# The start of a fused Macaron block re-ordered around its ternary weights, and its last store cut in two

## The reference

```python
x = x + 0.5 * ffn(layernorm(x), W_up, W_gate, W_down)
x = x + mamba(layernorm(x), ...)        # 1024 channels, 16 states, a scan over the tokens
x = x + 0.5 * ffn(layernorm(x), W_up, W_gate, W_down)

def ternary_quant(w):                   # once for each of the three matrices
    scale = mean(|w|) + 1e-8
    return clip(round(w / scale), -1, 1) * scale
def ffn(x, W_up, W_gate, W_down):       # 512 -> 2048 -> 512
    return (silu(x @ wu.T) * (x @ wg.T)) @ wd.T
```

## Time and profile before

| | us |
|---|---|
| median of three runs | 2939.0 (2936.71 to 2941.12) |
| the profiled execution | 2940.29 |
| its span, first to last instruction | 2938.7 |
| granted TensorE clock, mean | 0.970 |
| busy: PE / PEld / DVE / ACT / POOL | 2657.0 / 2054.0 / 2534.3 / 1900.3 / 2412.7 |
| first U begins | 54.44 |
| first down projection begins | 87.58 |
| last store issued | 2935.26 |

### The profile page before, as it was taken

How to read it: one execution, slowest core, us unless ns; L and a number is a source line. 1 busy time by engine, 2 the same in 40 slices (tenths; PEclk the granted TensorE clock), 3 DMA queues, 4 the chain that set the end, 5 groups by cost and what they waited for, 6 DMA issues and landing times.

```text
span 2938.7 us, 51656 instructions
## 1 busy us (share of the span) xinstructions
PE 2657.0 (90%) x17527; PEld 2054.0 (70%) x17527; DVE 2534.3 (86%) x3233; ACT 1900.3 (65%) x4428; POOL 2412.7 (82%) x2179
## 2 busy tenths in 40 slices
PE   4776899999999999999999999999999999999778
PEld 4555677776867777686777768677777867777555
DVE  6377899898889999898988989899998989899892
ACT  6375767666676766667676666767666676766651
POOL 1178888888898898989888898998989898897991
PEclk9888899999999999999999999999999999999898
DMA  7022222222222212222222131222213222221320
GB/s 261 31 60 69 62 53 69 49 53 72 51 70 53 70 46 55 73 51 69 53 65 50 48 80 44 71 58 64 51 49 79 48 69 57 65 51 48 87 55 15
DMA packets 91260, 185.22 MB, mean 63 GB/s; under 512 B 12220, under 2 KB 30456, under 8 KB 90488
## 3 DMA queue, kind: packets, MB, share of 16 engines
q1 hardware_dynamic: 72280, 113.76, 12.1%
q0 software_dynamic: 18720, 68.17, 11.8%
HBM read 104.82 MB, written 8.91 MB: 39 GB/s over the span
## 4 chain that ended last, share of the span: by engine, by line
PE 61%; POOL 12%; DVE 8%; ACT 5%; issue 5%; DMA 3%; POOLq 0%; DVEq 0%; ACTq 0%
PE ps L1560 20%; PE ps L1571 14%; PE ps L1583 10%; PE ps L1522 8%; POOL h L743 6%; PE ps L1632 5%; DVE h L1294 4%; DMA xw<-hc 3%; POOL hc L757 2%; PE ps L1593 2%; ACT ps L990 2%; DVE xc L1367 1%; POOL u L850 1%; POOL hl L842 1%; PE ps L1613 1%
## 5 line engine op out<-in xcount | busy, mean ns | idle before, releaser
L743 POOL TENSOR_TENSOR h<-u,bb 128x1024 f32<-128x1024 f32 x512 | 1247.1, 2436 | 82.5 <-PE ps L1522 36.7
L990 ACT ACTIVATE ps<-delta,a_neg 128x255 f32<-128x255 f32 x2048 | 877.0, 470 | 537.8 <-DVE h L1294 536.3
L1294 DVE TENSOR_TENSOR_SCAN h<-ps,h 128x512 f32<-128x512 f32 x1024 | 1189.5, 1203 | 27.3 <-ACT ps L990 13.2
L1560 PE MATMUL ps<-xh,q_up 128*128 128x256 f16 x2048 | 466.7, 275 | 38.0 <-DVE xl L1233 29.7
L1560 PE MATMUL ps<-xh,q_gate 128*128 128x256 f16 x2048 | 466.1, 274 | 28.4 <-DVE xw L1400 28.4
L1323 DVE SCALAR_TENSOR_TENSOR y<-ps,ccur,y 128x512 f32<-128x512 f32 x700 | 487.6, 737 | 1.7 <-PE ps L1522 1.1
L1522 PE MATMUL ps<-ident,h 128*128 128x128 f32 x3056 | 413.7, 278 | 64.0 <-DVE y L1323 58.8
L1560 PE MATMUL ps<-xl,q_up 128*128 128x256 f16 x2048 | 466.6, 275 | 0.0
L1560 PE MATMUL ps<-xl,q_gate 128*128 128x256 f16 x2048 | 465.5, 274 | 0.0
L1522 PEld LDWEIGHTS ps<-ident,h 128*128 128x128 f32 x3056 | 353.8, 142 | 135.4 <-issue 59.0
L842 POOL TENSOR_TENSOR hl<-act,hh 128x512 f16<-128x512 f32 x256 | 314.1, 1231 | 148.7 <-ACT hh L1015 148.7
(11 more groups left out here) (137 smaller groups left out, 3827.5 us busy)
## 6 DMA issues: line engine op xcount, KB each, us to landing
xw<-hc POOLq DMA_DIRECT2D x130, 512.0 KB, 4.5
bb<-b_scratch SPq DMA_DIRECT2D x224, 256.0 KB, 3.1
cplane<-c_scratch SPq DMA_DIRECT2D x130, 128.0 KB, 3.1
xs<-in_L_attn_resid_dram SPq DMA_DIRECT2D x17, 512.0 KB, 3.7
out_dram<-xs SPq DMA_DIRECT2D x16, 512.0 KB, 4.2
wraw<-in_L_ffn_W_up_dram SPq DMA_DIRECT2D x4, 1024.0 KB, 9.6
wraw<-in_L_ffn_W_gate_dram SPq DMA_DIRECT2D x4, 1024.0 KB, 12.5
wraw<-in_L_ffn_W_down_dram SPq DMA_DIRECT2D x4, 1024.0 KB, 14.1
```

Source lines behind the costliest of these rows:

```text
L743: pl.tensor_tensor(h[:, s % RING, :, :], u[:, :, :], bb[:, planes_of(s) % 2, s % PLANES:s % PLANES + 1, :].broadcast_to([P, HE, CH]), ALU. ...
L990: ins = ac.activation(abar[r][:, e, 1:], delta[:, k, 1:], ACT.Exp, scale=a_neg[:, k, n:n + 1])
L1294: v.tensor_tensor_scan(hr, abar[r].rearrange("p e t -> p (e t)"), hr, 0.0, ALU.mult, ALU.add).then_inc(scanned, 1)
L1560: ins = te.matmul(pp[:, f * CH:(f + 1) * CH], w[:, d, col:col + P], part[:, d, :], start=(d == 0 and part is xh), stop=(d == DB - 1 and pa ...
```

## The change

- **Half of the weights first.** The first up and gate pairs (0 to 3) need only the first halves of W_up and W_gate. TensorE now begins the fill when 12 of the 16 copies are there (both halves of W_up, the first of W_gate). It transposes W_gate's second half at the end of slot 1 (`HALF_SLOT`), behind U1_0 and G1_0. U1_4 waits for all 16 copies.
- **W_down's scale later.** `sum_abs(2, 3)` moves behind the tanh of U1_0; the four copies of W_gate's second half and the exponential of A_log (`second_half_saved`) move into slot 2, ahead of the tanh of U1_1; `scale(2)` becomes `scale_down` in slot 2 of VectorE, behind the gate product of pair 0. `sum_all(2)` and a wait for the scale stand ahead of G1_1, whose bank it borrows. The two `x_low` of VectorE move ahead of the ternary passes of W_gate's second half.
- **W_down in eight pieces** of 1024 columns, two in each of slots 2, 3 and 4 and one in each of 5 and 6 (`DOWN_AT`), with four PSUM banks for their transposes in place of two.
- **The drain has a table of its own**, `DRAIN_SLOTS`.
- **The last store in two**: in the drain, the 128 rows of DN2_0 are stored when it is evacuated, and those of DN2_1 after that one.
- `hidden_low` also waits for the former `hidden_low` (`hl_ready`), in every phase. `Z_ON_DVE` and `LOW_ON_DVE`, which could move GpSimd's work to VectorE, are empty.

```diff
+DRAIN_SLOTS = [ [("OM_0", 0, 4)], [], [], [], ["YT_2"], ["YT_3", ("OM_1", 0, 1)],
...
+    [("DN2_1", 0, 12), ("DN2_0", 9, 12)], [("DN2_0", 12, 16), ("DN2_1", 12, 16)], [], ]
-PLAN = {..., "drain": LOOP_SLOTS}
+PLAN = {..., "drain": DRAIN_SLOTS}
+Z_ON_DVE = []
+LOW_ON_DVE = {1: [], 2: []}
+DOWN_AT = [2, 2, 3, 3, 4, 4, 5, 6]
-        DOWN_SLOT = [SLOT_OF["fill"][f"G1_{r}"] for r in range(QUARTERS)]
+        HALF_SLOT, SCALE_SLOT = SLOT_OF["fill"]["G1_0"], SLOT_OF["fill"]["G1_1"]
+        DOWN_SLOT = DOWN_AT
# SP, store()
+                    if ph == "drain":
+                        sp.dma_start(out_dram[i - 1, :, t, :], xs[:, (i - 1) % XSLOTS, t, :]).then_inc(out_stored, 16)
+                if ph == "drain":
+                    return
# POOL, hidden_low()
                 need(pool, hh_ready, g + 1)
+                need(pool, hl_ready, g)
# ACT
             sum_abs(2, 2)
-            sum_abs(2, 3)
-            sc.wait_ge(alog_loaded, 16)
-            ac.activation(a_neg[:, :, :], a_neg[:, :, :], ACT.Exp).then_inc(a_exp, 1)
-            save_q(1, 1)
             sc.wait_ge(vec_step, 2)
-            sc.wait_ge(q_saved, UPGATE_SAVED)
+            def second_half_saved():
+                save_q(1, 1)
+                sc.wait_ge(alog_loaded, 16)
+                ac.activation(a_neg[:, :, :], a_neg[:, :, :], ACT.Exp).then_inc(a_exp, 1)
+                sc.wait_ge(q_saved, UPGATE_SAVED)
...
+                    if ph == "fill" and s == SCALE_SLOT:
+                        second_half_saved()
                     for name in results(ph, s, late=True):
                         evacuate(name)
+                    if ph == "fill" and s == HALF_SLOT:
+                        sum_abs(2, 3)
# DVE
-            ternary(1, 3, HALF_COLS, HALF_COLS)
             x_low("fill", -1, 1, 0)
             x_low("fill", -1, 1, 1)
-            scale(2)
+            ternary(1, 3, HALF_COLS, HALF_COLS)
...
+                    if ph == "fill" and s == SCALE_SLOT:
+                        scale_down()
...
+                    for r in range(2 * QUARTERS):
+                        if ph == "fill" and s == DOWN_SLOT[r]:
+                            ternary(2, 4 + r, r * F // 2, F // 2)
# PE
+                if ph == "fill" and name == "G1_1":
+                    sum_all(2)
+                    pe.wait_ge(scale_step, 7)
+                if ph == "fill" and p == PAIRS // 2:
+                    pe.wait_ge(q_saved, UPGATE_SAVED)
...
             ternary_T(1, 0)
-            ternary_T(1, 1)
-            sum_all(2)
-            pe.wait_ge(q_saved, UPGATE_SAVED)
-            pe.wait_ge(scale_step, 7)
+            pe.wait_ge(scale_step, 4)
+            pe.wait_ge(vcol_ready, 1)
+            pe.wait_ge(q_saved, UPGATE_SAVED - QB)
...
+                    if ph == "fill" and s == HALF_SLOT:
+                        ternary_T(1, 1)
+                    for r in range(2 * QUARTERS):
+                        if ph == "fill" and s - 1 == DOWN_SLOT[r]:
+                            ternary_down_T(r)
```

More of the change, by code:

```diff
@@ L199 @@
 ]
+DRAIN_SLOTS = [
+    [("OM_0", 0, 4)],
+    [],
+    [],
+    [],
+    ["YT_2"],
+    ["YT_3", ("OM_1", 0, 1)],
+    [("OM_1", 1, 2), ("OM_0", 4, 5)],
+    [("OM_0", 5, 8)],
+    [],
+    [],
+    [("OM_1", 2, 8)],
+    [],
+    [],
+    ["T2_0"],
+    [],
+    [],
+    ["T2_1"],
+    [],
+    ["U2_0", "G2_0"],
+    [],
+    ["U2_1"],
+    ["G2_1", "U2_2"],
+    ["G2_2"],
+    ["U2_3", "G2_3", "U2_4"],
+    [("DN2_0", 0, 3), "G2_4", "U2_5"],
+    [("DN2_0", 3, 6), "G2_5"],
+    [("DN2_0", 6, 8), "U2_6"],
+    [],
+    ["G2_6", "U2_7", ("DN2_0", 8, 9), "G2_7"],
+    [("DN2_1", 0, 12), ("DN2_0", 9, 12)],
+    [("DN2_0", 12, 16), ("DN2_1", 12, 16)],
+    [],
+]
 UG = {k: {f"{x}{k}_{p}" for x in "UG" for p in range(PAIRS)} for k in (1, 2)}
@@ L205 @@
 PHASES = {"fill": NEXT, "first": THIS | NEXT, "loop": PREV | THIS | NEXT, "last": PREV | THIS, "drain": PREV}
-PLAN = {"fill": FILL_SLOTS, "first": FIRST_SLOTS, "loop": LOOP_SLOTS, "last": LAST_SLOTS, "drain": LOOP_SLOTS}
+PLAN = {"fill": FILL_SLOTS, "first": FIRST_SLOTS, "loop": LOOP_SLOTS, "last": LAST_SLOTS, "drain": DRAIN_SLOTS}
 SLOTS, ORDER = {}, {}
@@ L558, in macaron_kernel @@
         q_banks = [ps[:, b, :] for b in range(4)]
-        sums, vecs = bank[free[0]], bank[free[1]]
+        sums = [bank[free[0]], bank[free[0]], bank[BANK_OF["fill"]["T1_1"]]]
+        vecs = bank[free[1]]
         QB = len(q_banks)
@@ L695, in _ @@
             phases(sp, run)
-            sp.wait_ge(out_stored, 16 * NCH)
+            sp.wait_ge(out_stored, 16 * (NCH - 1 + TB))
         @block.gpsimd
@@ L884, in run @@
                     for q in range(QT):
-                        if after(ph, f"YT_{q}", 0, s):
+                        if after(ph, f"YT_{q}", 0, s) and q not in Z_ON_DVE:
                             gated(ph, i, q)
                     for kind, p in hidden_units(ph, s):
-                        hidden_low(ph, i, kind, p)
+                        if p not in LOW_ON_DVE[kind]:
+                            hidden_low(ph, i, kind, p)
                     if after(ph, "DN1_1", 0, s):
@@ L953, in save_q_down @@
             def save_q_down(r):
[L955 to L959, removed]
+                b, d = r % 2, r // 2
+                sc.wait_ge(qt_ready, UPGATE_SAVED + r + 1)
+                ac.activation(q_down[:, 8 * b:8 * b + 8, d * P:(d + 1) * P],
+                              q_banks[r % QB].bitcast(f16).rearrange("p (f d) -> p f d", f=8), ACT.Copy,
+                              saturate=False).then_inc(q_saved, 1)
             for m in range(2):
@@ L1187, in run @@
                             conv_tanh(i, half)
[L1188 to L1191, removed]
+                    for r in range(2 * QUARTERS):
+                        if ph == "fill" and s - 1 == DOWN_SLOT[r]:
+                            save_q_down(r)
+                            if r == 2 * QUARTERS - 1:
+                                sc.wait_ge(q_saved, ALL_SAVED)
             phases(sc, run)
@@ L1249, in ternary @@
                 if piece >= 2:
-                    ve.wait_ge(qt_ready, QB * (piece - 1) if piece <= 5 else UPGATE_SAVED + 2 * (piece - 5))
+                    ve.wait_ge(qt_ready, QB * (piece - 1) if piece <= 5 else UPGATE_SAVED + piece - 5)
                 src, dst = wraw[m][:, lo:lo + cols], qh[:, piece % 2, 0:cols]
@@ L1262, in _ @@
             scale(0)
+            v.tensor_scalar(tanh_sc[:, :], wscale[:, 0:1], -0.5 / XN_SCALE, None, ALU.mult).then_inc(vec_step, 1)
             for part in range(2):
@@ L1412, in run @@
                         scan_of(*step)
+                    for kind, p in hidden_units(ph, s - 1):
+                        if p in LOW_ON_DVE[kind]:
+                            hidden_low(ph, i, kind, p)
                     if s == MASK_H and "IN_0" in PHASES[ph]:
@@ L1488, in sum_all @@
                 pe.wait_ge(asum_ready, m + 1)
-                te.matmul(sums[:, m:m + 1], ones[:, :], asum1[:, m:m + 1], start=True, stop=True).then_inc(asums_ready, 1)
+                te.matmul(sums[m][:, m:m + 1], ones[:, :], asum1[:, m:m + 1], start=True, stop=True).then_inc(asums_ready, 1)
             def ternary_T(m, part):
@@ L1505, in ternary_down_T @@
                 pe.wait_ge(q_ready, 4 + r + 1)
[L1506 to L1510, removed]
-                        ins = te.transpose(q_banks[b].bitcast(f16)[:, j * P:(j + 1) * P],
-                                           qh[:, r % 2, f * P:(f + 1) * P], ident16[:, :])
-                    ins.then_inc(qt_ready, 1)
+                if r >= QB:
+                    pe.wait_ge(q_saved, UPGATE_SAVED + r - QB + 1)
+                for j in range(8):
+                    ins = te.transpose(q_banks[r % QB].bitcast(f16)[:, j * P:(j + 1) * P],
+                                       qh[:, r % 2, j * P:(j + 1) * P], ident16[:, :])
+                ins.then_inc(qt_ready, 1)
             def states_T(i, s):
@@ L1694, in run @@
                             job(ph, i, name, lo, hi)
-                    if ph == "fill" and s - 1 in DOWN_SLOT:
-                        ternary_down_T(DOWN_SLOT.index(s - 1))
+                    if ph == "fill" and s == HALF_SLOT:
+                        ternary_T(1, 1)
+                    for r in range(2 * QUARTERS):
+                        if ph == "fill" and s - 1 == DOWN_SLOT[r]:
+                            ternary_down_T(r)
                     step = step_of(ph, i, s)
```

31 lines of the change are left out of this document (19 added, 12 removed).

## The result

The kernel after took 2946.8 us (median of 10 runs, 2940.3 to 2951.5), the kernel before 2940.0 (10 runs, 2936.6 to 2944.0). The ratio is 1.0021, with a 95% interval of 1.0012 to 1.0030. I had forecast 2938.1 and a range up to 2943.0. The profiled execution took 2944.9 us, with a span of 2943.3, which is 4.6 us more than before. Single executions of one kernel scatter by some 0.2%, so the two spans alone decide nothing. What decides is the ten runs of each, and the places of the trace where a difference comes back in every pass of the loop.

A forecast was written before the change was run, and what follows sets the result against it. PE was taken to bound the fill from its first U on, and the loop. Fill -0.5, store -0.7 and `hidden_low` wait +0.3 gave -0.9 us, so 2938.1 against the median of 2939.0, range 2932.5 to 2943.

The forecast's parts named there:

- part 7: Wait in `hidden_low`: 5.6 us of POOL (2.6 single waits, 3 pairs), of which 0.3 arrives, bounds 0 and 12.8.
- part 3: Fill: PE waits for W_down's pieces and the shared port; down projection at 87.1 (84.8 to 88.8), 0.5 us earlier.
- the whole head start: Rival in the fill: PE never waits for W_down, -5.4 - 0.7, so 2932.9 us; chance 0.10.
- paid in full: Rival on the wait in `hidden_low`: 12.8 us of POOL reach the end, 2950.6 us; chance 0.06.
- Parts 1 to 3: Fill: first U 7.9 us earlier, W_down's pieces from 58.1, PE then waiting; down projection 0.5 us earlier.
- Part 5: Drain's own table: same jobs in the same order, same instructions, so nothing.
- Part 6: Last store in two: the second half has half the bytes to move, 0.7 us less, bounds 0 and 1.35.
- Part 4: Smaller edits of the fill (`x_low`, W_out's load, GpSimd's edges): nothing; if the cover fails, 1.1 us.
- VectorE never held: Rival in the fill: GpSimd never holds VectorE out, down projection 2.8 us earlier, 2935.8 us; chance 0.12.
- always held: Rival in the fill: VectorE waits at every meeting with GpSimd, down projection at 88.8, 2939.8 us; chance 0.22.

The follow-up runs named there:

- b_wait_rest: The kernel before with the new wait on `hl_ready` in every `hidden_low` except the second of a pair: 2941.2 us, ratio 1.0002.
- b_wait: The kernel before with the new wait on `hl_ready` in all 256 `hidden_low`: 2943.1 us, ratio 1.0006.
- a_nowait: The changed kernel without the new wait on `hl_ready` in `hidden_low`: 2939.4 us, ratio to before 0.9997.
- a_low_dve: The changed kernel with the second `hidden_low` of both pairs moved from GpSimd to VectorE: 2998.1 us, ratio 1.0200.

## Why the prediction was wrong, step by step

**The step that failed is part 7.** It had the mechanism and the count right: the single waits free, two pairs in a chunk. Two sizes were off. A pair costs 0.19 us and not 0.1, 5.3 us in all where I had 3 for the pairs. Of the 2.6 us for the single waits nothing shows: with them alone (b_wait_rest) the shortest chunk is 170.79 against 170.76, and the ratio 1.0002. The larger error was the share that arrives, 0.3 us of 5.6: "of which I let 0.3 arrive (bounds 0 and 12.8), for in the loop PE is busier than POOL". Of the 0.38 us of the two pairs, 0.35 to 0.51 arrive in the chunks of the kernel after (sixth, seventh, shortest) and 0.31 in b_wait, so all or nearly all. I had argued from busy shares, and they don't tell where an engine is waited for. The row that could have told it was there: in every chunk PE stands idle 0.9 us for `xw`, that waits for a DMA, and that for `hc` on GpSimd, whose order runs back through the first pair without a wait longer than 0.2 us other than on its own results. The share of POOL in the chain, 12%, is 350 us; it had to be asked in which stretch these lie, and whether the pairs stand in it. The price of a pair stood there too. GpSimd before, at the start of the seventh chunk, waiting for its own product just ahead:

```profile
1007.11 2.35 POOL L743 TENSOR_TENSOR h<-u,bb 128x1024 f32<-128x1024 f32 x1 [0.20 <-POOL u L850]
```

With 0.19 a pair in full, the sum is -0.3 - 0.8 + 5.3 = +4.2. That the profiled difference is +4.6 is partly luck, since two spans of one kernel differ by more; the medians differ by 6.8, with an interval of 3.5 to 8.8, and +4.2 lies in it.

Two slips of the text change nothing: `hl` ends 1.0 us behind the pass in part 3 and not 1.1, and the whole head start leaves out the +0.3 of the loop that the other cases have.

**The rival "paid in full"** was the nearest one, with the right mechanism at 0.06, and too dear, at 12.5 us for waits most of which are free.

**Parts 1 to 3, the fill**, came out as forecast in kind. The first U started at 46.92 (46.55 forecast), G1_1 waited 0.34 for the ones matmul (0.7), VectorE's first ternary pass of W_down began at 58.04 (58.1), and the down projection at 87.35 (87.1, in 84.8 to 88.8). The clock stayed at half level into the second job (0.67 over 46.9 to 52.0). Yet the 0.2 us can't be called measured from one pair of traces. With the fill of before, the first down projection began between 87.22 and 88.60 in seven profiled runs, 88.1 in the mean; with the fill of after between 86.89 and 87.98 in six, 87.4 in the mean. That is 0.7 us earlier, where 0.5 was forecast. At the mark of slot 1 both lie between 155.2 and 157.9.

**The meetings at the port** happened in both directions, and in the first ternary pass too. DVE and POOL of the kernel after:

```profile
60.03 0.75 DVE L1304 TENSOR_SCALAR w_out<-wraw,thr 128x1024 f16<-128x1024 f32 x1
60.81 2.06 DVE L1306 SCALAR_TENSOR_TENSOR w_out<-wraw,thr,w_out 128x1024 f16<-128x1024 f32 x1
...
73.09 1.68 DVE L1304 TENSOR_SCALAR w_out<-wraw,thr 128x1024 f16<-128x1024 f32 x1
74.81 1.28 DVE L1306 SCALAR_TENSOR_TENSOR w_out<-wraw,thr,w_out 128x1024 f16<-128x1024 f32 x1
```

```profile
60.14 1.65 POOL L886 TENSOR_TENSOR hl<-act,hh 128x512 f16<-128x512 f32 x1
...
73.07 1.15 POOL L886 TENSOR_TENSOR hl<-act,hh 128x512 f16<-128x512 f32 x1 [1.76 <-ACT hh L1062]
```

The second pass takes 1.28 us alone and 2.06 with an `hl` in it, the first 0.75 alone and 1.68. At 73.07 `hl` keeps its 1.15 us, and the pass that starts 0.02 us later ends 0.55 us behind it: about its own length, so it hadn't begun. The Trainium skill (GPSIMD Engine Reference, Specifications) lets GpSimd contend with 2-port modes as well as with two SBUF inputs. On this the trace of before was silent; the trace of after agrees, in that the first pass, with one input from SBUF, is held too (1.68 us instead of 0.75).

**Part 5** held: the drain has the same jobs in the same order. **Part 6** held: 0.8 us measured, 0.7 forecast. Part 4 showed no cost.

**The rivals of the fill** (VectorE never held, always held, the head start whole) spread over some 7 us, and I gave them 0.44 in all. The loop, where 28 repetitions of a tenth of a us decide, had 0.06. The bound that I had stated, "if the loop's length changes by more than 2 us", is the one that broke.

## What to carry to other kernels

A cost that is repeated in each pass of a loop is priced by where it stands, not by the busy share of its engine: follow its lateness from its place through the waits (here `hc`, its DMA, VectorE's add, PE's gate job) until one of them has slack, and take it in full if none has. A wait on the instruction just ahead on the same engine wasn't free, even where the two are independent: 0.19 us for each pair here, while the waits with other instructions between cost nothing measurable. Time taken out of a loop comes back only up to the next place where its engine waits for others, so here additions cost more than removals brought.

## What the runs showed that I had not expected

**Two things go with the long chunks.** One is a transfer. The DMA of `hc` that is issued 17.1 us behind the mark lands 4.4 to 4.7 us later in the quiet chunks and up to 6.1 in others, and VectorE's add and PE's gate job come late by the difference. VectorE in a_nowait, in its seventh chunk (170.80 us) and in its ninth (173.16), then windows over the two chunks:

```profile
1022.93 0.69 DVE L1453 TENSOR_TENSOR xw<-ps,xw 128x512 f32<-128x512 f32 x1 [1.50 <-DMA xw<-hc]
1367.40 0.69 DVE L1453 TENSOR_TENSOR xw<-ps,xw 128x512 f32<-128x512 f32 x1 [2.78 <-DMA xw<-hc]
```

```profile
1001.20:1172.00 170.80, 161.19 (x1086) 125.01 (x1085) 155.74 (x201) 115.72 (x274) 150.80 (x136) 1.00 0.24 60
1344.38:1517.54 173.16, 161.28 (x1085) 124.85 (x1084) 155.80 (x201) 115.71 (x274) 150.78 (x136) 1.00 0.24 59
```

The granted clock is 1.00 in both and PE is busy for the same time, so a chunk can be 2.4 us longer without a fall of the clock; 1.3 us of it stand at this DMA. The other thing is the clock. Two windows of 10 us in a chunk of the kernel before that took 174.2 us, in which that DMA landed in time (4.46 us):

```profile
1450.00:1460.00 10.00, 6.36 (x42) 4.68 (x40) 10.00 (x14) 3.40 (x7) 9.03 (x7) 0.86 0.19 51
1460.00:1470.00 10.00, 10.00 (x67) 8.36 (x66) 9.60 (x15) 6.34 (x16) 6.96 (x8) 0.80 0.27 65
```

PE had been idle for 2.73 us at 1455.83, waiting for `xc`. Behind such a stop the granted clock falls for part of many chunks, quiet ones too, to 0.83 in one window, and here it is low in two. In the twelve kernels other than a_low_dve every chunk in which it was low for twice as long or more as in the quiet ones was 2.0 us or more above the shortest of its run. The two things don't explain all: chunks with neither reached 1.7 us above. Why the DMA lands late at times isn't shown. How often all this happens differs from run to run, and so two profiled spans of one kernel can differ by several us. A change of 0.2% is read from the quiet chunks, and confirmed by the medians.

**A store of half the size.** The last stores in the view of the DMA issues (KB each, us from issue to landing), before and after:

```profile
out_dram<-xs SPq DMA_DIRECT2D x1, 512.0 KB, 2.8
```

```profile
out_dram<-xs SPq DMA_DIRECT2D x2, 256.0 KB, 2.0
```

So 256 KB less are 0.8 us less, and if the time goes with the size, 1.2 us of both don't depend on it.
